# Two mixture-of-experts stages and what stands between them: order of scores, routing, biases and projections

## The chip, the cores and the metric

The kernel runs on one core of a Trainium2 chip: TensorE (PE, with its weight loads PEld), VectorE (DVE), ScalarE (ACT), GpSimd (POOL), and SyncE (SP), which issues most transfers. The metric is the device time of one execution in microseconds. The kernel before has a median of 1687.51 us over three runs (1680.59 to 1689.58).

## The reference, cut to what matters

Eight layers run one after the other on 2048 tokens of 128 features in float32, each on the output of the one before: a state-space block, 32 experts, causal attention, eight experts, windowed attention, a linear layer with ternary weights, a test-time-training block, seven experts with a shared one. Ahead of each layer the rows are normalised. The parts the change touches:

```
# eight experts, capacity 160, one expert a token
probs = softmax(x @ router_w + router_b); e = argmax(probs)
tokens of e that fit:  relu(x @ w1[e] + b1[e]) @ w2[e] + b2[e]
left-over tokens:      relu(x @ ow1 + ob1) @ ow2 + ob2
# ternary layer
y = x @ sign_with_threshold(weight).T * alpha + bias
# test-time training (Ttt): queries, keys, values by one projection,
# two gradient steps on a small gated network, then the queries through it
# seven experts, the two best of each token, plus a shared expert
w, idx = top_k(softmax(x @ router_w), 2), made to sum to 1
y = sum_k w_k * (silu(x @ w_gate[idx_k]) * (x @ w_up[idx_k])) @ w_down[idx_k]
    + (silu(x @ sw_gate) * (x @ sw_up)) @ sw_down
```

## The kernel before, in words

Every stage is a class with one method for each engine (pe, dve, act, pool, sp). The engines run their own lists of instructions in the order written out by hand and meet on semaphores. Waits.wait_ge puts a wait in an engine's list; mark and own are the waits of DVE and POOL on their own earlier results. The 2048 tokens are 16 tiles of 128 rows, handled as four chunks of four tiles. At each stage's start ChunkNorm (line 349) takes roots on ACT, a reciprocal and three tiles a chunk on DVE (line 369) and the fourth tile on POOL; ChunkFeatures (line 401) transposes a chunk on PE (line 418) into one of two PSUM banks and ACT copies it (line 428), so that tokens lie along the free axis. A float32 matmul shows as two instructions on PE.

**Eight experts (Moe8).** PE transposes all four chunks, waits for the ends of the stage before and makes the 16 score matmuls into bank 2 (line 2562). DVE adds the router bias, takes the largest score and subtracts it (2590 to 2595), ACT takes Exp (2681), DVE sums, divides, finds the largest of each tile (max, 2604) and its index (max_index, 2607). Dispatch (line 1032) marks the chosen expert, PE counts with a triangular matrix (1051, 1052), DVE makes row numbers, and POOL scatters 16 tiles with indirect DMAs (1116) into HBM. Beside that PE runs the dense layer of the left-over tokens over all rows: hidden (2570) and output (2521), c = 0 to 3, DVE and ACT evicting. DVE adds the output to X, first a sum into tmp (2619), then one update for each tile (2624), and signals ox. Only at ox = 4 does PE turn the scattered rows (rows_pe, 2530) for the first expert; hidden_pe (2540), the ReLUs (DVE 2655, ACT 2696) and out_pe (2552) follow for eight experts, the results go back by indirect DMA.

**Ternary.** PE puts the bias into each of four banks with a matmul of one row (bias_pe, 2757), transposes chunks and adds the product of each chunk (2765). DVE adds to X and takes statistics for the next norm, chunk by chunk.

**Ttt.** PE transposes chunks 0 and 1, then makes the projections of tiles 0 to 3, transposes chunk 2, projects tiles 6 and 7, transposes chunk 3, and so on (line 3060). DVE adds the key bias (3170), ACT copies values (3352), queries (3355) and squares (3347); ACT's copy of the transposed keys of chunk 0 is line 3438, and the first gradient step begins with a Sigmoid (3365).

**Seven experts (Moe7).** The tokens of each expert are laid out in blocks of 256 rows, NB = 22 of them ("e"), and the shared expert has eight blocks ("s") over all tokens. The order of blocks is:

```
self.blocks = [("s", s) for s in range(F)] + [("e", j) for j in range(NB)] + [("s", s) for s in range(F, 8)]
```

with F = FRONT = 6, so two shared blocks stand behind the experts. The list of PE: four chunks of transposes, 16 score matmuls into bank 7 (3691), the up-projections of a block in two groups of eight instructions (3662), the down product of the block before (3674), and after the third group the two counting matmuls (3681, 3682). DVE: choose_dve (3720 to 3733) with max and max_index for each tile, place_dve (3743 to 3781) with weigh_dve inside, then the products silu(gate) * up (mul_dve, 3808) and additions to X (home_dve, 3817). For the first two blocks (EARLY = 2) ACT copies the up half out of PSUM (3873) and POOL multiplies (3919) in DVE's place, while DVE routes. POOL then issues 32 scatters (3931), SP loads the rows of a block (3606), PE turns them (3633). At the end the experts' results lie in HBM, SP reads them back in four parts (3610), DVE adds them (3826, 3828) and SP writes the output (3613).

## Time and profile before

| | |
|---|---|
| median of three runs | 1687.51 us (1680.59 to 1689.58) |
| profiled execution | 1679.48 us, its span 1677.4 us |
| TensorE granted clock, mean | 0.886 |
| busy: PE, DVE, ACT, POOL | 1264.7, 982.8, 669.4, 659.1 us |
| chain that ended last | PE 51%, DVE 13%, POOL 12%, issue 10%, DMA 6%, ACT 5%, SP's queue 3% |

Times in the rows below are counted from the span's start. Durations come from the one profiled execution. Its 2.1 us outside the span are start and end of the program. The clock column has 1.00 for 2.4 GHz and 0.50 for 1.2 GHz. "idle 2.05 <-DVE" in brackets means that the engine stood idle for so long before the instruction and that DVE ended it.

### The profile page before, as it was taken

Reading aid. Unit: us, or ns where it says so; the run is one execution under the profiler, and the core shown is the slowest. Engines: PE = TensorE matmul, PEld = TensorE weight load, DVE = VectorE, ACT = ScalarE, POOL = GpSimd, SP = SyncE. Lnnn points to the kernel's source line nnn. Section 1 sums busy time; section 2 is a strip of 40 time slices with the busy share of each in tenths; the row PEclk is TensorE's granted clock in tenths of the full one; section 3 lists DMA queues with packets and bytes.
Section 4 is the critical chain, followed back from the end, with each engine's and each line's share of the span. In section 5 each row is a group of like instructions: output and inputs, shape, how many; then the busy total and the mean of one; then the engine's idle time right before and its main releaser. Section 6 shows DMA issues by size and latency. Waiting matters only on the chain.

```text
span 1677.4 us, 23947 instructions
## 1 busy us (share of the span) xinstructions
PE 1264.7 (75%) x8790; PEld 761.1 (45%) x8790; DVE 982.8 (59%) x1746; ACT 669.4 (40%) x1253; POOL 659.1 (39%) x647
## 2 busy tenths in 40 slices
PE   5467677531684668788778489979988998994997
PEld 2123332320453224434357234445555556683997
DVE  7899899860111988878453554366545554551333
ACT  3754233120353347767722335643323323231432
POOL 1288878377576430000034200025512440054443
PEclk9679899756897769989979699989999999996999
DMA  6257568011332422211001322150000000001112
GB/s 221 104 178 265 209 232 276 18 50 51 88 94 83 163 95 68 64 47 29 9 27 30 123 92 61 38 217 4 1 0 1 0 1 1 1 25 46 48 39 92
DMA packets 75445, 133.80 MB, mean 80 GB/s; under 512 B 12723, under 2 KB 39670, under 8 KB 74688
## 3 DMA queue, kind: packets, MB, share of 16 engines
q1 hardware_dynamic: 66400, 115.97, 20.9%
q0 software_dynamic: 8064, 13.87, 2.5%
q10 hardware_dynamic: 864, 2.43, 0.4%
q8 instruction: 70, 1.15, 0.3%
q14 instruction: 47, 0.39, 0.1%
HBM read 96.22 MB, written 38.38 MB: 80 GB/s over the span
## 4 chain that ended last, share of the span: by engine, by line
PE 51%; DVE 13%; POOL 12%; issue 10%; DMA 6%; ACT 5%; SPq 3%; POOLq 0%; DVEq 0%; ACTq 0%
PE ps L3662 6%; PE ps L1752 5%; POOL sb_arena L1018 5%; POOL xe L1116 3%; PE ps L3674 3%; PE ps L2119 2%; PE ps L644 2%; DVE sb_arena L1818 2%; ACT sb_arena L2066 2%; PE ps L2102 2%; PE ps L2973 2%; PE ps L2970 2%; PE ps L2962 1%; PE ps L2964 1%; DMA sb_arena<-xe 1%
## 5 line engine op out<-in xcount | busy, mean ns | idle before, releaser
L1818 DVE TENSOR_REDUCE sb_arena<-ps 128x2 f32<-128x1024 f32 (+2 forms) x192 | 211.1, 1130 | 60.7 <-PE ps L2347 34.2
L2066 ACT ACTIVATE sb_arena<-ps 128x512 f32<-128x512 f32 (+1 forms) x320 | 160.3, 554 | 58.6 <-PE ps L2119 54.9
L644 PE MATMUL ps<-sb_arena,sb_const 128*128 128x512 f32 x256 | 136.2, 677 | 27.9 <-DVE sb_arena L837 27.9
L831 DVE TENSOR_TENSOR_SCAN sb_arena<-ps,sb_arena 128x1024 f32<-128x1024 f32 x64 | 144.9, 2279 | 4.9 <-ACT ps L926 3.9
L1850 POOL CAST sb_arena<-sb_arena 128x8 bf16<-128x8 f32 (+2 forms) x32 | 6.5, 204 | 293.1 <-DVE sb_arena L1818 149.9
L1752 PE MATMUL ps<-sb_arena 128*32 128x256 f32 (+3 forms) x1856 | 117.6, 361 | 0.4 <-ACT sb_arena L2300 0.2
L3808 DVE TENSOR_TENSOR sb_arena<-sb_arena,ps 128x512 f32<-128x512 f32 x56 | 38.4, 687 | 111.8 <-PE ps L3662 111.8
L1116 POOL DMA_INDIRECT xe<-sb_arena x80 | 79.9, 999 | 51.0 <-issue 30.5
L644 PEld LDWEIGHTS ps<-sb_arena,sb_const 128*128 128x128 f32 x256 | 56.1, 221 | 93.5 <-issue 53.5
L1018 POOL TENSOR_TENSOR sb_arena<-sb_Wreg,sb_arena 128x1024 f32<-128x1024 f32 x32 | 79.0, 2490 | 40.3 <-DMA sb_arena<-bcrows 32.1
L3514 POOL TENSOR_TENSOR sb_arena<-sb_arena 128x512 f32<-128x512 f32 x32 | 40.7, 1270 | 137.2 <-DVE sb_arena L3192 137.2
L1478 POOL DMA_INDIRECT y<-sb_arena x80 | 77.7, 972 | 37.5 <-ACT sb_arena L1432 20.1
L3662 PE MATMUL ps<-sb_arena 128*128 128x256 f32 x352 | 85.2, 385 | 0.5 <-ACT sb_arena L3855 0.5
L2119 PE MATMUL ps<-sb_arena 51*128 51x256 bf16 (+2 forms) x768 | 61.7, 253 | 28.2 <-ACT sb_arena L2066 27.8
L1018 POOL TENSOR_TENSOR sb_arena<-sb_arena 128x1024 f32<-128x1024 f32 x32 | 74.6, 2355 | 19.5 <-DMA sb_arena<-bcrows 14.8
L2102 PE MATMUL ps<-sb_arena 55*128 55x128 bf16 (+4 forms) x576 | 63.6, 298 | 18.5 <-DVE sb_arena L1818 11.9
L2300 ACT ACTIVATE sb_arena<-ps 128x768 f32<-128x768 f32 x64 | 50.3, 786 | 62.7 <-PE ps L2369 62.7
L617 PE MATMUL ps<-sb_arena,sb_constb 96*128 96x512 bf16 x96 | 31.0, 406 | 57.1 <-DVE sb_arena L837 50.4
L3940 POOL DMA_INDIRECT y<-sb_arena x44 | 43.0, 976 | 76.5 <-ACT sb_arena L3863 69.8
L3662 PEld LDWEIGHTS ps<-sb_arena 128*128 128x128 f32 x352 | 64.6, 193 | 8.5 <-ACT sb_arena L3855 0.9
L926 ACT ACTIVATE ps<-sb_arena 128x1024 f32<-128x1024 f32 x32 | 35.8, 1118 | 77.2 <-DVE sb_arena L831 77.1
L837 DVE TENSOR_TENSOR sb_arena<-sb_arena,ps 128x1024 f32<-128x1024 f32 x48 | 58.6, 1221 | 12.2 <-PE ps L617 6.1
(479 smaller groups left out, 2856.0 us busy)
## 6 DMA issues: line engine op xcount, KB each, us to landing
sb_arena<-bcrows SPq DMA_DIRECT2D x80, 512.0 KB, 6.4
xe<-sb_one SPq DMA_DIRECT2D x31, 260.0 KB, 8.9
sb_Wreg<-e0w SPq DMA_DIRECT2D x24, 256.0 KB, 7.2
sb_arena<-xe SPq DMA_DIRECT2D x16, 325.0 KB, 3.1
y<-sb_zero SPq DMA_DIRECT2D x20, 256.0 KB, 6.7
sb_arena<-y SPq DMA_DIRECT2D x4, 1024.0 KB, 9.1
sb_Wreg<-e1w SPq DMA_DIRECT2D x16, 256.0 KB, 2.7
sb_Wreg<-e3gu SPq DMA_DIRECT2D x1, 4096.0 KB, 12.5
```

The source lines that it names most:

```text
L644: t = e.matmul(k.b(self.Y + c), k.c("ident"), self.hc[i % 4][:, c * 512:(c + 1) * 512], start=False, stop=n == 15)
L831: e.tensor_tensor_scan(self.hh[i % 3], k.pair(2 * (i % 2)).rearrange("p c t -> p (c t)"), self.dB[i % 3], 0.0, MUL, ADD).then_inc(S.scan.s ...
L837: e.tensor_tensor(self.two(self.hc[i % 4]), self.two(self.hh[i % 3]), k.pair(self.C), MUL).then_inc(S.hcv.sem, 1)
L1018: e.tensor_tensor(self.dB[i % 3], self.du[b][:, eb, :], self.Bs[i % 4], MUL).then_inc(S.dB.sem, 1)
L1116: e.indirect_dma_start(buf, bass.IndirectOffsetOnAxis(self.iw[:, c:c + 1], 0), xn[q][:, i, :], None, bounds_check=rows - 1, oob_is_err=Fal ...
L1478: e.indirect_dma_start(self.y, bass.IndirectOffsetOnAxis(at, 0), self.ob[u % 3][:, c, :], None, bounds_check=8191, oob_is_err=False).then_ ...
L1752: t = e.matmul(k.b(self.sum_bank(qc))[32 * j:32 * j + 32, o:o + wd], self.vaug[:, b * 8 + kt, 4 * hg + j, :], self.PT[x][:, j, a - q0:a - ...
L1818: e.tensor_reduce(dst, src, AX.X, MAX).then_inc(S.mxr.sem, 1)
L2066: e.activation(self.PT[s % 4][:, 2 * h:2 * h + 2, 0:n], bank[:, :, 0:n], ACT.Exp, scale=self.scale).then_inc(S.ex.sem, 1)
L2102: t = e.matmul(view[:, p, a:z], Q[r, j % 2, tok], KK[r, j % 2, k0 + a:k0 + z], start=True, stop=True, skip_group_check=True)
L2119: t = e.matmul(banks[h][:, j, a:z], KK[r, j, kt * 128:(kt + 1) * 128], Q[r, j, q0 + a:q0 + z], start=True, stop=True, skip_group_check=True)
L3662: t = e.matmul(k.b(2 * (n % 2) + which)[:, 256 * q:256 * (q + 1)], self.matrix(which, block, 2 * (n % 2) + q), src, start=True, stop=True)
```

## The change

In Moe8 the scores are made chunk by chunk between the transposes, in banks 6 and 7 (half of the tiles each), and routing runs by halves: shift of half 0, its Exp and maxima, shift of half 1, indices of half 0, maxima and indices of half 1. The scores of the second half wait for signal od of the stage before. Turning rows no longer waits for ox = 4 but for the evictions of the left-over layer; hidden_pe waits for a new signal ov, the sum into tmp. ACT takes the root of chunk 3 after the first copy of features. In Ternary the bias of bank 3 moves behind the output of chunk 2. In Ttt the projections of tiles 0 to 3 go ahead of chunk 1's transposes, and ACT's copy of the keys goes ahead of the last value copy, the last query copy behind the last root. In Moe7 scores are made by chunks, in two parts of 12 and 4 tiles, and DVE chooses in these parts; PE counts right after the scores, ACT takes the Exp ahead of its copy of the rows, EARLY with its copies and POOL products goes away, and FRONT is 7.

```diff
@@ -2514,7 +2514,7 @@
         w.wait_ge(S.oha, 2 * c + 2)
-        w.wait_ge(S.ox, c - 1)
+        w.wait_ge(S.ov, c - 1)
         for j in range(4):
@@ -2524,7 +2524,8 @@
         w.wait_ge(S.rows, 16)
-        w.wait_ge(S.ox, 4)
+        w.wait_ge(S.ohv, 8)
+        w.wait_ge(S.oha, 8)
         w.wait_ge(S.xT, ex - 1)
@@ -2533,6 +2534,7 @@
         w.wait_ge(S.xT, ex + 1)
+        w.wait_ge(S.ov, 4)
         for g in range(2):
@@ -2552,15 +2554,30 @@
+    def scores(self, h):
+
+        return self.k.b(6 + h)[:, 0:8 * self.E]
+
+    def scores_pe(self, e, w, c):
+        k, E = self.k, self.E
+        self.f.wait(w, c)
+        for j in range(4):
+            i, o = 4 * c + j, (4 * (c % 2) + j) * E
+            t = e.matmul(self.scores(c // 2)[:, o:o + E], self.xnT[:, i * 128:(i + 1) * 128], k.s("rw1"), start=True, stop=True)
+        return t
+
     def pe(self, e, w):
         k, S, E = self.k, self.S, self.E
-        self.f.pe(e, w, self.ln.wait_rows)
+        self.f.chunk_pe(e, w, self.ln.wait_rows, 0)
+        self.scores_pe(e, w, 0)
+        self.f.chunk_pe(e, w, self.ln.wait_rows, 1)
+        self.f.chunk_pe(e, w, self.ln.wait_rows, 2)
+        self.scores_pe(e, w, 1).then_inc(S.lg.sem, 1)
+        self.f.chunk_pe(e, w, self.ln.wait_rows, 3)
         w.all(self.before.ends)
-        lg = k.b(2)[:, 0:NT * E]
-        for i in range(NT):
-            self.f.wait(w, i // 4)
-            t = e.matmul(lg[:, i * E:(i + 1) * E], self.xnT[:, i * 128:(i + 1) * 128], k.s("rw1"), start=True, stop=True)
-        t.then_inc(S.lg.sem, 1)
+        w.wait_ge(self.before.S.od, 16)
+        self.scores_pe(e, w, 2)
+        self.scores_pe(e, w, 3).then_inc(S.lg.sem, 1)
         self.disp.pe(e, w)
@@ -2582,29 +2599,50 @@
+    def half(self, h):
+
+        tiles = slice(8 * h, 8 * h + 8)
+        return tiles, self.p.rearrange("p (i e) -> p i e", e=self.E)[:, tiles], lambda v: v[:, tiles].unsqueeze(2).to_broadcast([128, 8, self.E])
+
+    def shift_dve(self, e, w, h):
+        S, E = self.S, self.E
+        tiles, p3, bc = self.half(h)
+        w.wait_ge(S.lg, h + 1)
+        w.mark(e.tensor_tensor(p3, self.scores(h).rearrange("p (i e) -> p i e", e=E),
+                               self.k.s("rb1").unsqueeze(1).to_broadcast([128, 8, E]), ADD))
+        w.own()
+        w.mark(e.tensor_reduce(self.mx[:, tiles], p3, AX.X, MAX))
+        w.own()
+        e.tensor_tensor(p3, p3, bc(self.mx), SUB).then_inc(S.shift.sem, 1)
+
+    def best_dve(self, e, w, h):
+        S = self.S
+        tiles, p3, bc = self.half(h)
+        w.wait_ge(S.probs, h + 1)
+        w.mark(e.tensor_reduce(self.sm[:, tiles], p3, AX.X, ADD))
+        w.own()
+        w.mark(e.reciprocal(self.sm[:, tiles], self.sm[:, tiles]))
+        w.own()
+        w.mark(e.tensor_tensor(p3, p3, bc(self.sm), MUL))
+        w.own()
+        for i in range(8):
+            t = e.max(self.v8[:, 8 * h + i, :], p3[:, i, :])
+        w.mark(t)
+
+    def which_dve(self, e, w, h):
+        tiles, p3, bc = self.half(h)
+        w.own()
+        for i in range(8):
+            t = e.max_index(self.i8[:, 8 * h + i, :], self.v8[:, 8 * h + i, :], p3[:, i, :])
+        w.mark(t)
+
     def route_dve(self, e, w):
...
+        self.shift_dve(e, w, 0)
+        self.best_dve(e, w, 0)
+        self.shift_dve(e, w, 1)
+        self.which_dve(e, w, 0)
+        self.best_dve(e, w, 1)
+        self.which_dve(e, w, 1)
         w.own()
@@ -2616,9 +2654,9 @@
         w.own()
-        w.mark(e.tensor_tensor(self.tmp.rearrange("p (j d) -> p j d", j=4), bo.rearrange("p (j d) -> p j d", j=4),
-                               self.b2[:, 1024:1152].unsqueeze(1).to_broadcast([128, 4, 128]), ADD))
-        w.own()
+        e.tensor_tensor(self.tmp.rearrange("p (j d) -> p j d", j=4), bo.rearrange("p (j d) -> p j d", j=4),
+                        self.b2[:, 1024:1152].unsqueeze(1).to_broadcast([128, 4, 128]), ADD).then_inc(S.ov.sem, 1)
+        w.wait_ge(S.ov, c + 1)
         for j in range(4):
@@ -2674,11 +2712,16 @@
         k, S = self.k, self.S
-        self.ln.act(e, w, self.before.S.stats, (2, 3))
-        self.f.act(e, w)
+        ready = self.before.S.stats
+        self.ln.act(e, w, ready, (2,))
+        self.f.chunk_act(e, w, 0)
+        self.ln.act(e, w, ready, (3,))
+        for c in range(1, 4):
+            self.f.chunk_act(e, w, c)
         w.all(self.before.ends)
-        w.wait_ge(S.shift, 1)
-        e.activation(self.p, self.p, ACT.Exp).then_inc(S.probs.sem, 1)
+        for h in range(2):
+            w.wait_ge(S.shift, h + 1)
+            e.activation(self.p[:, 64 * h:64 * h + 64], self.p[:, 64 * h:64 * h + 64], ACT.Exp).then_inc(S.probs.sem, 1)
         for c in range(4):
@@ -2775,13 +2818,13 @@
         self.bias_pe(e, 2)
-        self.bias_pe(e, 3)
         self.f.chunk_pe(e, w, self.ln.wait_rows, 1)
...
         self.out_pe(e, w, 2)
+        self.bias_pe(e, 3)
         self.out_pe(e, w, 3)
@@ -3062,10 +3105,10 @@
         self.f.chunk_pe(e, w, self.ln.wait_rows, 0)
-        self.f.chunk_pe(e, w, self.ln.wait_rows, 1)
         w.wait_ge(S.g_w, 16)
...
         self.qkv_pe(e, w, range(0, 4))
+        self.f.chunk_pe(e, w, self.ln.wait_rows, 1)
         self.f.chunk_pe(e, w, self.ln.wait_rows, 2)
@@ -3432,11 +3475,11 @@
         self.root_act(e, w, 2)
-        self.value_act(e, w, 3)
-        self.query_act(e, 3)
         w.wait_ge(S.ktp, 1)
         e.copy(self.kT[:, 0:512], k.b(0)).then_inc(S.kT.sem, 1)
+        self.value_act(e, w, 3)
         self.root_act(e, w, 3)
+        self.query_act(e, 3)
         for step in range(2):
@@ -3548,7 +3591,9 @@
-    BLK, NB, FRONT, EARLY = 256, 22, 6, 2
+    BLK, NB, FRONT = 256, 22, 7
+
+    PARTS = [(0, 12, 4), (12, 16, 5)]
     ROWS = BLK * NB
...
@@ -3653,9 +3697,7 @@
             src = self.xT[m % 3]
-        if 2 <= n < 2 + 2 * self.EARLY:
-            w.wait_ge(S.uc, n - 1)
-        elif n >= 2:
+        if n >= 2:
             self.wait_h(w, n - 2)
@@ -3681,15 +3723,27 @@
+    def scores_pe(self, e, w, c):
+
+        k = self.k
+        self.f.wait(w, c)
+        bank = k.b(self.PARTS[c // 3][2])
+        for i in range(4 * c, 4 * c + 4):
+            t = e.matmul(bank[:, i * 8:(i + 1) * 8], self.xnT[:, i * 128:(i + 1) * 128], k.s("rw3"), start=True, stop=True)
+        return t
+
     def pe(self, e, w):
         k, S = self.k, self.S
-        self.f.pe(e, w, self.ln.wait_rows)
+        self.f.chunk_pe(e, w, self.ln.wait_rows, 0)
+        self.f.chunk_pe(e, w, self.ln.wait_rows, 1)
+        self.scores_pe(e, w, 0)
+        self.f.chunk_pe(e, w, self.ln.wait_rows, 2)
+        self.scores_pe(e, w, 1)
+        self.scores_pe(e, w, 2).then_inc(S.lg.sem, 1)
+        self.f.chunk_pe(e, w, self.ln.wait_rows, 3)
+        self.scores_pe(e, w, 3).then_inc(S.lg.sem, 1)
         w.all(self.before.ends)
-        lg = k.b(7)[:, 0:128]
-        for i in range(NT):
-            self.f.wait(w, i // 4)
-            t = e.matmul(lg[:, i * 8:(i + 1) * 8], self.xnT[:, i * 128:(i + 1) * 128], k.s("rw3"), start=True, stop=True)
-        t.then_inc(S.lg.sem, 1)
+        self.count_pe(e, w)
         w.wait_ge(k.g_w["e3"], 32)
@@ -3700,8 +3754,6 @@
                 self.turn_pe(e, w, self.blocks[v + 1][1])
-            if v == 1:
-                self.count_pe(e, w)
             self.up_pe(e, w, 2 * v + 1)
@@ -3716,18 +3768,19 @@
         v8, i8 = self.v8, self.i8
-        w.wait_ge(S.lg, 1)
...
+        for x, (a, z, bank) in enumerate(self.PARTS):
+            w.wait_ge(S.lg, x + 1)
+            w.mark(e.tensor_copy(self.p[:, 8 * a:8 * z], k.b(bank)[:, 8 * a:8 * z]))
+            w.own()
+            w.mark(e.tensor_copy(p3[:, a:z, 7], k.c("padneg").to_broadcast([128, z - a])))
+            w.own()
+            for i in range(a, z):
+                t = e.max(v8[:, i, :], p3[:, i, :])
+            w.mark(t)
+            w.own()
+            for i in range(a, z):
+                t = e.max_index(i8[:, i, :], v8[:, i, :], p3[:, i, :])
+            w.mark(t)
         w.own()
@@ -3834,12 +3887,10 @@
         last = len(self.blocks)
-        for v in range(self.EARLY):
-            self.home_dve(e, w, v)
-        for v in range(self.EARLY, last):
+        for v in range(last):
             for n in (2 * v, 2 * v + 1):
                 self.mul_dve(e, w, n)
-            if v > self.EARLY and self.blocks[v - 1][0] == "s":
+            if v and self.blocks[v - 1][0] == "s":
                 self.home_dve(e, w, v - 1)
@@ -3868,15 +3919,19 @@
         e.activation(self.sg[y], k.b(2 * y), ACT.Silu).then_inc(S.sg.sem, 1)
-        if n < 2 * self.EARLY:
-            w.wait_ge(S.mu, n + 1)
-            e.copy(self.uc[y], k.b(2 * y + 1)).then_inc(S.uc.sem, 1)
...
         k, S = self.k, self.S
-        self.ln.act(e, w, self.before.S.stats)
-        self.f.act(e, w)
+        ready = self.before.S.stats
+        self.ln.act(e, w, ready, (0, 1, 2))
+        self.f.chunk_act(e, w, 0)
+        self.f.chunk_act(e, w, 1)
+        self.ln.act(e, w, ready, (3,))
+        self.f.chunk_act(e, w, 2)
+        self.f.chunk_act(e, w, 3)
         w.all(self.before.ends)
+        w.wait_ge(S.shift, 1)
+        e.activation(self.d, self.d, ACT.Exp).then_inc(S.probs.sem, 1)
         self.ln.wait_rows(w, 3)
@@ -3885,9 +3940,6 @@
             self.silu_act(e, w, 2 * v)
-            if v == 0:
-                w.wait_ge(S.shift, 1)
-                e.activation(self.d, self.d, ACT.Exp).then_inc(S.probs.sem, 1)
             if more and v >= self.FRONT:
@@ -3911,13 +3963,6 @@
             e.tensor_copy(self.xq[q].bitcast(I32)[:, :, 128], k.c("places").rearrange("p (i q) -> p q i", q=2)[:, q]).then_inc(S.ids.sem, 1)
-        for n in range(2 * self.EARLY):
-            v, y = n // 2, n % 2
-            w.wait_ge(S.sg, n + 1)
-            w.wait_ge(S.uc, n + 1)
-            w.wait_ge(S.o, v - 2)
-            e.tensor_tensor(self.h[v % 3][:, 2 * y:2 * y + 2, :], self.sg[y].rearrange("p (q t) -> p q t", q=2),
-                            self.uc[y].rearrange("p (q t) -> p q t", q=2), MUL).then_inc(S.hp.sem, 1)
         self.ln.wait_rows(w, 3)
```

## Rows read from the trace of the kernel before

**Rows 1.** Chain that ended last, routing of the eight experts: start, length, what

```profile
846.47 6.64 PE ps L2562 x32
...
858.07 2.28 DVE sb_arena L2607 x17
```

**Rows 2.** Timeline there: start, length, engine, line, operation, [idle before <-releaser]

```profile
853.23 0.29 DVE L2590 TENSOR_TENSOR sb_arena<-ps,sb_small 128x128 f32<-128x128 f32 x1 [7.73 <-PE ps L2562]
...
854.27 1.28 ACT L2681 ACT_TABLE_LOAD   x1 [7.18 <-DVE sb_arena L2595]
855.57 0.31 ACT L2681 ACTIVATE sb_arena<-sb_arena 128x128 f32<-128x128 f32 x1
...
856.84 1.19 DVE L2604 MAX8 sb_arena<-sb_arena 128x8 f32<-128x8 f32 x16
...
892.84 1.14 DVE L2624 SCALAR_TENSOR_TENSOR sb_X<-sb_arena,sb_X 128x128 f32<-128x128 f32 x4
...
894.12 0.47 PE L2530 MATMUL ps<-sb_const,sb_arena 80*128 80x80 f32 x4 [2.05 <-DVE sb_X L2624]
...
895.69 0.67 DVE L2655 TENSOR_SCALAR sb_arena<-ps,sb_small 128x160 f32<-128x160 f32 x2 [1.71 <-PE ps L2540]
```

**Rows 3.** Windows, ternary stage: stretch, length, busy times, TensorE clock, DMA share, GB/s

```profile
1092.00:1094.00 2.00, 2.00 (x4) 0.65 (x2) 1.90 (x12) 0.36 (x2) 1.38 (x2) 0.50 0.00 0
```

**Rows 4.** Timeline of the ternary stage and the start of Ttt

```profile
1091.29 3.52 PE L2757 MATMUL ps<-sb_Wreg,sb_const 1*128 1x512 f32 x4
...
1092.35 1.01 DVE L369 TENSOR_SCALAR sb_Wreg<-sb_X,sb_ln,sb_rs 128x128 f32<-128x128 f32 x3
...
1094.75 1.11 PE L418 MATMUL ps<-sb_const,sb_Wreg 128*128 128x128 f32 x4
...
1105.65 1.10 PE L418 MATMUL ps<-sb_const,sb_arena 128*128 128x128 f32 x4 [2.07 <-DVE sb_arena L369]
...
1114.78 0.69 DVE L3170 TENSOR_TENSOR sb_arena<-ps,sb_small 128x512 f32<-128x512 f32 x1 [3.61 <-PE ps L3060]
...
1122.49 0.61 ACT L3438 COPY sb_arena<-ps 128x512 f32<-128x512 f32 x1
```

**Rows 5.** Timeline of the seven experts, up to the first rows turned

```profile
1467.22 1.35 PE L418 MATMUL ps<-sb_const,sb_arena 128*128 128x128 f32 x8 [2.12 <-DVE sb_arena L369]
...
1468.41 4.96 PE L3691 MATMUL ps<-sb_small,sb_arena 128*128 128x8 f32 x32
...
1478.22 0.42 DVE L3746 TENSOR_REDUCE sb_arena<-sb_arena 128x128 bf16<-128x256 f32 x1
...
1480.80 0.29 DVE L3749 COPY sb_arena<-ps 128x128 f32<-128x128 f32 x1 [0.94 <-PE ps L3682]
...
1481.66 3.94 POOL L3919 TENSOR_TENSOR sb_arena<-sb_arena 128x512 f32<-128x512 f32 x3 [2.35 <-ACT sb_arena L3873]
...
1481.98 1.11 DVE L3757 TENSOR_TENSOR sb_arena<-sb_arena 128x128 f32<-128x128 f32 x1
...
1488.26 1.11 POOL L3931 DMA_INDIRECT xe<-sb_arena  x1 [2.66 <-DVE sb_arena L3774]
...
1533.22 0.66 PE L3633 MATMUL ps<-sb_const,sb_arena 128*128 128x128 f32 x2 [25.54 <-DMA sb_arena<-xe]
...
1534.35 3.78 PE L3662 MATMUL ps<-sb_arena 128*128 128x256 f32 x8 [0.46 <-ACT sb_arena L3855]
```

**Rows 6.** Chain that ended last, the two blocks behind the experts

```profile
1658.46 6.91 PE ps L3662 x32
1665.37 3.58 PE ps L3674 x32
```

**Rows 7.** Timeline of the end

```profile
1664.60 2.01 SPq L3610 DMA_DIRECT2D sb_arena<-y  x4
...
1669.32 0.68 DVE L3826 TENSOR_TENSOR sb_X<-sb_X,sb_arena 128x512 f32<-128x512 f32 x1
```

**Rows 8.** Source line 3610, the four reads of expert rows at the end

```profile
DMA to landing us min/median/max: 3.9/5.4/6.8
```

More of the change, by code:

```diff
@@ L2470, in __init__ @@
         self.S = S = k.signals(
-            g_w=16, stats=4, ids=1, **chunk_signals(), **dispatch_signals(), lg=1, shift=1, probs=1,
-            scat=256, oh=16, ohv=8, oha=8, od=4, ox=4, rows=16, tr=8, xT=8, mg=16, hv=16, ha=16, o=8, oa=8, row0=64, row1=64, row2=64, row3=64, back0=16, back1=16, back2=16, back3=16)
+            g_w=16, stats=4, ids=1, **chunk_signals(), **dispatch_signals(), lg=2, shift=2, probs=2,
+            scat=256, oh=16, ohv=8, oha=8, od=4, ov=4, ox=4, rows=16, tr=8, xT=8, mg=16, hv=16, ha=16, o=8, oa=8, row0=64, row1=64, row2=64, row3=64, back0=16, back1=16, back2=16, back3=16)
         self.put = [S.row0, S.row1, S.row2, S.row3]
@@ L2602, in route_dve @@
         w.own()
-        for i in range(NT):
-            w.mark(e.max(self.v8[:, i, :], p3[:, i, :]))
-        w.own()
-        for i in range(NT):
-            w.mark(e.max_index(self.i8[:, i, :], self.v8[:, i, :], p3[:, i, :]))
+        for i in range(8):
[3 more added lines that the diff above has]
+        tiles, p3, bc = self.half(h)
+        w.own()
+        for i in range(8):
+            t = e.max_index(self.i8[:, 8 * h + i, :], self.v8[:, 8 * h + i, :], p3[:, i, :])
+        w.mark(t)
+    def route_dve(self, e, w):
+        self.shift_dve(e, w, 0)
[4 more added lines that the diff above has]
+        self.which_dve(e, w, 1)
         w.own()
@@ L3562, in __init__ @@
         self.S = S = k.signals(
-            **chunk_signals(), lg=1, shift=1, probs=1, chosen=1, cnt=1, eid=1, iw=1, gu=NB, dn=NB, ids=2, wts=2, xq=1, scat=512,
-            **{f"load{i}": 16 * ((NB + 5 - i) // 6) for i in range(6)}, tr=NB, xT=NB, mg=60, mu=60, sg=60, uc=2 * self.EARLY, hp=2 * self.EARLY, h=60 - 2 * self.EARLY, o=30, oa=2 * NB, ox=8,
+            **chunk_signals(), lg=2, shift=1, probs=1, chosen=1, cnt=1, eid=1, iw=1, gu=NB, dn=NB, ids=2, wts=2, xq=1, scat=512,
+            **{f"load{i}": 16 * ((NB + 5 - i) // 6) for i in range(6)}, tr=NB, xT=NB, mg=60, mu=60, sg=60, h=60, o=30, oa=2 * NB, ox=8,
             **{f"row{i}": 32 * ((NB + 3 - i) // 4) for i in range(4)}, **{f"back{c}": 16 for c in range(4)}, fin=4, out=64)
@@ L3586, in __init__ @@
         self.xT = [A.take(256) for _ in range(3)]
-        self.sg, self.uc = [A.take(512) for _ in range(2)], [A.take(512) for _ in range(2)]
+        self.sg = [A.take(512) for _ in range(2)]
         self.h = [B.take(1024).rearrange("p (b t) -> p b t", b=4) for _ in range(3)]
@@ L3615, in wait_h @@
     def wait_h(self, w, n):
-        early = 2 * self.EARLY
-        w.wait_ge(*((self.S.hp, n + 1) if n < early else (self.S.h, n + 1 - early)))
+        w.wait_ge(self.S.h, n + 1)
     def wait_out(self, w, v):
@@ L3718, in choose_dve @@
         v8, i8 = self.v8, self.i8
-        w.wait_ge(S.lg, 1)
-        w.mark(e.tensor_copy(self.p, k.b(7)[:, 0:128]))
-        w.own()
-        w.mark(e.tensor_copy(p3[:, :, 7], k.c("padneg").to_broadcast([128, NT])))
-        w.own()
-        for i in range(NT):
-            t = e.max(v8[:, i, :], p3[:, i, :])
-        w.mark(t)
-        w.own()
-        for i in range(NT):
-            t = e.max_index(i8[:, i, :], v8[:, i, :], p3[:, i, :])
-        w.mark(t)
+        for x, (a, z, bank) in enumerate(self.PARTS):
[11 more added lines that the diff above has]
+            w.mark(t)
         w.own()
```

11 lines of the change are left out of this document (removed).

## The prediction

> **What bounds the kernel now.** I read the chain that ended last, stage by stage, then the timeline where the diff touches it, then the end. One core runs the stages in a row and the chain hardly leaves them, so what counts is how much earlier each touched stretch hands on. In the stage of eight experts PE makes 32 passes of scores (two for each of 16 matmuls) after all transposes, 6.64 us, and DVE then routes until 860.35 [rows 1] with PE idle. The stage of seven experts has the same pattern: 4.96 us of scores, DVE's routing, the first of 32 scatters on POOL at 1488.26, and PE, out of work, waits 25.54 us for the rows that it turns at 1533.22 [rows 5]. The path there is scores, routing, POOL, DMA, not PE. At the end two blocks of the shared expert run on PE while the rows are read back [rows 6, 7].
>
> **Eight experts, scores and routing.** A pass took 6.64 / 32 = 0.21 us [rows 1]. Eight passes now fall into PE's wait for chunk 1's rows, eight more go between the transposes of chunks 2 and 3, where some 0.6 us of waiting was; the last score is ready 1.66 + 0.6 = 2.2 us sooner, near 850.9, the first half's near 846.9. DVE starts there: three operations of at most 0.29 us [rows 2], 0.8. The Exp waits for ACT's last copy of features, which moves to about 848.1 (846.9 with 0.6 each for chunk 3's transposes and the copy), and for its table, 1.28 [rows 2]; it ends at 849.65. From then DVE works without a wait: sum, reciprocal, product and eight maxima 1.35 (16 maxima took 1.19 [rows 2]), the second half's shift 0.8, eight indices 1.15 (half of 2.28 [rows 1]), the second half's product and maxima 1.35, its indices 1.15. That is 5.8 us, to 855.5, where it was 860.35. Eight more small instructions are in it. Bounds: 2.2 (halving pays nothing beyond the earlier scores) and 5.5 (half the width, less time). I take **4.7**. The 16 scatters and the left-over tokens' layer start earlier by the same. The new wait of the scores for signal od costs nothing: those copies are over before the last transposes.
>
> **Rows turned early.** PE stood 2.05 us between the last left-over product and the transposes, for DVE's sum and its four updates of X; the first hidden matmul came 0.7 later [rows 2]. Now PE turns at 892.1, and only the hidden layer waits for the sum, which ended at 892.8: 2.0 us earlier. But the updates (1.14 us from 892.84) stand ahead of DVE's first ReLU, which moves from 895.69 to 894.0 only [rows 2]. I take **1.7**, bounds 0 and 2.0.
>
> **Ternary stage.** Biases 2 and 3, four passes, took 3.52 us ahead of chunk 1's transposes at 1094.75 [rows 4]; its rows were ready at 1093.4 (DVE's three, 1.01 us from 1092.35 [rows 4]). With bias 2 alone (half, 1.76) PE turns then. Bias 3 moves behind output 2, where DVE's additions and statistics are the bound. PE ran at half its clock here [rows 3], so chunk 1's output may come 0.2 late. I take **1.2**, bounds 0.5 and 1.4.
>
> **Ttt stage.** The first eight passes of the projections stood behind chunk 1's transposes at 1105.65, before which PE was idle for 2.07, and need only chunk 0 [rows 4]. Its transposes ended at 1105.65 - 2.07 = 1103.6; with ACT's copy of 0.6 the passes start at 1104.2, 1.4 before chunk 1. Its transposes come later than now, but chunk 2's (the next wait for DVE) do not, and the keys of chunk 1 follow from 1114.78 [rows 4] on the same path. Bounds 0.5 and 2.5. The copy of kT (0.61 us [rows 4]) goes ahead and the query copy last; PE and the sigmoid's table now wait for that one. It costs 0.2, at most 0.6, at best nothing. Net **1.2**.
>
> **Seven experts, up to the scatters.** Before chunks 2 and 3 PE stood idle for 2.12 us; the scores ended at 1473.37, a pass costing 0.155 [rows 5]. Eight passes (1.2 us) go into that hole and chunk 2's transposes start 0.8 earlier, since ACT no longer has the last root ahead of chunk 0's copy: last score near 1471.4, first 24 passes near 1469.2. DVE takes 12 tiles first: copies 0.45, maxima 0.9, indices 1.7 (by the 1.19 and 2.28 for 16 [rows 1, 2]), to 1472.4, then four tiles with their copies in 1.5, to 1473.9 instead of 1477.5. So the reduce at 1478.22 [rows 5] moves by 3.6, its result from 1478.64 to 1475.05. DVE went on only at 1480.80 [rows 5], since the counting matmuls stood behind three groups of up-projections. Now PE counts at once, and what comes last is the Exp: shift 1474.25, table 1.28, Exp and three weight operations 0.9, so 1476.5: **4.3** gained. Behind it an addition of 128 elements took 1.11 us [rows 5] where such an operation takes 0.29 [rows 2], and two more like it (1.13, 1.25) ended with POOL's products, three in 3.94 us [rows 5]. The change takes these products off POOL: 3.49 - 0.87 = **2.6**, bounds 0 and 2.8. The first scatter moves 6.9 us, to 1481.4, and all up to 1533.22 with it, to 1526.3.
>
> Cover for the seven front blocks: DVE starts their products behind its routing, so PE pauses after two groups until 1481.8. A block is (6.91 + 3.58) / 2 = 5.24 us [rows 6]; six and a last product end near 1515, 11 us before the rows land.
>
> **The end.** One block less behind the experts takes 5.24 us off PE, but the rows' reads were issued at 1664.60 [rows 7] and landed 3.9 to 6.8 us later [rows 8]: the first at 1668.5, and the first addition ran at 1669.32 [rows 7]. The reads become the bound. I take **0.4**, bounds 0 and 0.8.
>
> **Where the skill speaks against it.** The activation began 0.02 us after its table load of 1.28 [rows 2]. The Trainium skill, "ScalarE: Activation LUTs", What ACT_TABLE_LOAD costs, puts a switch of tables at about 2.66 us with a drain. By that both Exps, which would end DVE's last wait, came 1.4 later and the sum would be 13.3 instead of 16.1; the row decides.
>
> **Sum.** 4.7 + 1.7 + 1.2 + 1.2 + 6.9 + 0.4 = 16.1 us, against the profiled execution's 1679.48: 1663.4. The runs shown have the median 1687.51 and lie from 1680.59 to 1689.58, so the profiled one is as fast as the fastest. From the median the sum gives 1671.4, from the middle of all four executions (1684.0) 1667.9; I forecast 1670. About 0.5% (8.4 us) is what a measurement here can tell from no change.
>
> **Rivals.**
> - The last block pays in full (5.2 instead of 0.4): 1665. For it: PE was the chain to 1668.95. Against: the landing at 1668.5. Chance 0.07.
> - A faster clock: PE, busier ahead of each routing, is not cut to half (the rows at 1534.35 took 3.78 for eight passes, 1.73 at full clock [rows 5, 6]). Three such stretches of 4 to 5 us give 2 each: 1664. Against: PE still idles 6 us and more in each. 0.10.
> - Half gains: the split pays only the 2.2, and POOL's products were not what stretched DVE: 16.1 - 2.5 - 2.6 = 11, so 1676. For it, the halves' handovers between ACT and DVE. 0.14.
> - The change does not do what it says: DVE gets the first scores only when ACT and PE are nearly through, another wait (copy of the rows for POOL, now behind the Exp) holds the scatters. 5 to 8 us left: 1681. The copy starts at 1475.8, 4 us ahead of its need. 0.07.
> - Slower: the front blocks become the bound. They must end by 1526.3, which a mean of over 6.7 us a block breaks. At half clock a block takes 11 us (3.78 for eight passes [rows 5], the down product doubled): 7 x 5.8 us more, less the 11 spare, puts 30 us on the forecast: 1700. Against: before, the same blocks ran on at 5.24 after pauses of 1 us. The Trainium skill, "TensorE: Matmul & The Clock Gate", A second HAM failure mode: psum-queue depth-cycling, has the clock swing when PE idles briefly between groups; by that rule this case is the outcome. 0.03.
>
> My forecast keeps 0.59. Faster by over 0.5%: 0.59 + 0.07 + 0.10 + 0.14 less some spread of the runs, 0.88; same 0.09; slower 0.03. The range 1657 to 1682 reaches from the faster rivals on a fast run to half gains on a slow one.
>
> **What would show it.** After: DVE's first routing operation of the eight experts starts before the scores end, and DVE has no wait over 1 us after the Exp; first rows turned right behind the last left-over product; three short additions of 0.29 instead of 1.1; first scatter about 7 us earlier within its stage; PE's idle time ahead of the rows near 11 instead of 25.5; additions at the end waiting for the DMA. Wrong would be: PE at work on shared blocks when the rows land, or a scatter that waits for ACT.

## The result, and the profile after

The changed kernel took 1658.22 us, median of four runs (1655.43 to 1661.09), against 1684.05 for the kernel before (four runs): ratio 0.9856, 95% interval 0.9828 to 0.9885. The forecast was 1670 with a range of 1657 to 1682. The gain is 24 to 26 us where the steps sum to 16. The profiled execution took 1655.43, its span 1653.6 (before: 1679.48 and 1677.4), mean clock 0.892 instead of 0.886.

To find where it came from, the same instruction is looked up in both traces at each stage's seam, and the starts subtracted. What changes from one seam to the next is that stretch's part. In the table "third" is a later trace of the same changed kernel (after_third, below); both stand against the one trace of before.

| stretch | forecast | first trace | third |
|---|---|---|---|
| start to causal attention (code unchanged) | 0 | +0.8 | +3.2 |
| causal attention (unchanged) | 0 | -6.7 | +1.0 |
| eight experts, scores and routing | -4.7 | -4.4 | -4.3 |
| its rows turned | -1.7 | -1.9 | -2.0 |
| window attention (unchanged) | 0 | -2.8 | +1.6 |
| ternary | -1.2 | -0.9 | -0.8 |
| start of Ttt | -1.2 | -0.8 | -1.5 |
| seven experts up to the first scatter | -6.9 | -6.7 | -7.7 |
| end | -0.4 | -1.0 | -1.0 |
| sum of the changed parts | -16.1 | -15.7 | -17.3 |

Small rests between the stretches (up to 0.6) are left out. So the parts came close to the forecast, except the end. The rest of the first trace's 23.9 us, some 8, lies in stages that the change does not touch.

The timeline of the changed kernel in the eight experts, where before all scores stood behind all transposes [rows 1, 2]; columns are start, duration, engine and line, operation, and in brackets the idle time before it with its releaser:

```profile
839.52 1.71 PE L2566 MATMUL ps<-sb_small,sb_arena 128*128 128x8 f32 x8
841.37 0.22 DVE L2611 TENSOR_TENSOR sb_arena<-ps,sb_small 128x64 f32<-128x64 f32 x1 [1.74 <-PE ps L2566]
841.97 3.42 PE L2566 MATMUL ps<-sb_small,sb_arena 128*128 128x8 f32 x16
842.22 0.59 ACT L428 COPY sb_arena<-ps 128x512 f32<-128x512 f32 x1 [1.87 <-PE ps L418]
842.82 1.28 ACT L2724 ACT_TABLE_LOAD   x1
844.11 0.26 ACT L2724 ACTIVATE sb_arena<-sb_arena 128x64 f32<-128x64 f32 x1
844.40 0.22 DVE L2622 TENSOR_REDUCE sb_arena<-sb_arena 128x8 f32<-128x64 f32 x1 [2.30 <-ACT sb_arena L2724]
...
881.94 0.50 PE L2531 MATMUL ps<-sb_const,sb_arena 80*128 80x80 f32 x4 [1.22 <-DMA sb_arena<-xe]
```

DVE starts before the second half's scores are made, waits once, for the table and the Exp, and works without a wait from 844.40 on. The last line is the first turning of rows: what ended PE's wait there is now the load of the rows, no longer DVE's updates of X [rows 2].

The seven experts, which answers to [rows 5]:

```profile
1450.13 2.51 PE L3732 MATMUL ps<-sb_small,sb_arena 128*128 128x8 f32 x16
1452.74 0.26 DVE L3773 COPY sb_arena<-ps 128x96 f32<-128x96 f32 x1 [1.56 <-PE ps L3732]
1458.37 0.42 DVE L3799 TENSOR_REDUCE sb_arena<-sb_arena 128x128 bf16<-128x256 f32 x1
1458.93 0.26 PE L3723 MATMUL ps<-sb_arena,sb_constb 128*128 128x128 bf16 x1 [2.80 <-DVE sb_arena L3799]
1459.59 0.17 DVE L3841 TENSOR_SCALAR sb_arena<-sb_arena 128x16 f32<-128x16 f32 x1 [0.80 <-ACT sb_arena L3934]
1461.36 0.28 DVE L3810 TENSOR_TENSOR sb_arena<-sb_arena 128x128 f32<-128x128 f32 x1
1464.89 1.10 POOL L3976 DMA_INDIRECT xe<-sb_arena  x1 [13.49 <-DVE sb_arena L3827]
1510.15 0.66 PE L3677 MATMUL ps<-sb_const,sb_arena 128*128 128x128 f32 x2 [13.08 <-DMA sb_arena<-xe]
```

PE now makes the scores of 12 of the 16 tiles ahead of the last chunk's transposes (the first line is the second and third chunk's), DVE's wait for the Exp is 0.80, the addition that took 1.11 us takes 0.28, the counts no longer stand behind up-projections, and PE waits 13.08 us for the rows instead of 25.54. Seven blocks fit ahead of them.

The end, answering to [rows 7]: the reads are issued at 1641.03, and DVE waits for them with no work left on PE. SPq is SP's queue.

```profile
1639.95 2.02 PE L3716 MATMUL ps<-sb_Wreg,sb_arena 128*128 128x128 f32 x16 [0.90 <-DVE sb_arena L3861]
1641.03 2.01 SPq L3655 DMA_DIRECT2D sb_arena<-y  x4
1644.94 0.69 DVE L3879 TENSOR_TENSOR sb_X<-sb_X,sb_arena 128x512 f32<-128x512 f32 x1 [2.51 <-DMA sb_arena<-y]
```

The causal attention, in four stretches. First the kernel before, then the changed one (stretch, its length, then busy time and instructions of PE, PEld, DVE, ACT and POOL, granted clock, DMA share, GB/s):

```profile
592.00:620.00 28.00, 19.41 (x170) 7.50 (x169) 23.54 (x27) 10.08 (x19) 8.00 (x14) 0.50 0.38 125
700.00:727.00 27.00, 22.61 (x263) 10.55 (x254) 18.81 (x30) 15.55 (x32) 1.62 (x8) 0.75 0.12 37
```

```profile
592.00:620.00 28.00, 18.07 (x181) 7.17 (x182) 24.98 (x29) 11.33 (x22) 9.10 (x14) 0.59 0.38 129
700.00:727.00 27.00, 21.12 (x305) 11.31 (x309) 22.34 (x34) 18.74 (x38) 1.62 (x8) 1.00 0.18 56
```

In the same 27 us PE got through 305 instructions instead of 263: before, it had been cut to 1.2 GHz for part of the stretch, after, it ran at 2.4 GHz throughout. This gave 4.5 us, and the earlier return to 2.4 GHz near 615 gave 2.2: the starts of PE's matmuls shift at these two places and at no other in the stage. The code there is the same, so the question for the runs was whether this belongs to the program.

### The profile page after: what moved, and what is told of

It reads as the page before. It is cut to its first block, busy times and chain, and to the rows that moved or that the text cites. A ratio compares the mean times of both kernels' runs of the same rounds, so it can differ in the third digit from the quotient of the medians.

```text
span 1653.6 us, 23951 instructions
## 1 busy us (share of the span) xinstructions
PE 1258.6 (76%) x8790; PEld 759.5 (46%) x8790; DVE 987.0 (60%) x1758; ACT 666.1 (40%) x1249; POOL 651.7 (39%) x643
## 4 chain that ended last, share of the span: by engine, by line
PE 49%; DVE 14%; POOL 12%; issue 11%; DMA 6%; ACT 5%; SPq 3%; POOLq 0%; DVEq 0%; ACTq 0%
PE ps L1752 5%; PE ps L3704 5%; POOL xe L1116 4%; POOL sb_arena L1018 3%; PE ps L644 3%; DVE sb_arena L1818 3%; PE ps L3716 2%; PE ps L2119 2%; ACT sb_arena L2066 2%; DVE sb_arena L831 2%; PE ps L2102 2%; DMA sb_arena<-xe 2%; PE ps L3016 2%; PE ps L3013 2%; PE ps L3005 1%
## 5 line engine op out<-in xcount | busy, mean ns | idle before, releaser
L1752 PE MATMUL ps<-sb_arena 128*32 128x256 f32 (+3 forms) x1856 | 113.0, 350 | 0.4 <-ACT sb_arena L2300 0.2
```

What stands on the lines that cost most here:

```text
L1752: t = e.matmul(k.b(self.sum_bank(qc))[32 * j:32 * j + 32, o:o + wd], self.vaug[:, b * 8 + kt, 4 * hg + j, :], self.PT[x][:, j, a - q0:a - ...
```

## The experiments

Theories: **P**, the change speeds the untouched stages; **U**, they swing from execution to execution. There are twelve runs, in three groups of four; each group had one chip for all its kernels, named B, C and D below. A stands for the result and the first two traces, whose chip is not on record.

**Chip B: both kernels again.** before_again and after_again have no edit.

> The kernel before, unchanged, for a second trace. In the first two traces the causal attention, whose code the change does not touch, took 7.1 us less after the change (its clock fell for some 15 us near 712 before, and did not after) and the window attention 2.8 us less. Theory U (these stages swing from run to run, and the parts that were changed give only 15 to 16 us): this trace shows a causal attention that differs from the first one's 224.8 us (608.5 to 833.3) by several us. Theory P (it goes with the program): 224.8 within 1.5 us again. Ratio 1.000 within 0.3%.

> The changed kernel, for a second trace. Theory P: causal attention 218.1 us again (within 1.5), total 24 to 26 us below the kernel before. Theory U: causal attention anywhere from 218 to 225, and a total of 15 to 26 us below. The changed stretches themselves should repeat within 0.5 us each: 4.4 routing of eight experts, 1.9 rows turned, 1.7 ternary and start of Ttt, 6.7 seven experts up to the scatters, 0.9 end.

Measured: before_again 1713.62 (ratio 0.9999, interval 0.9976 to 1.0021); after_again 1704.12 against 1712.06, ratio 0.9953 (0.9923 to 0.9982). The gain fell from 24 us to 8, and both kernels are slower than on A, by 30 and by 46 us. Neither theory had this. The trace of after_again shows why, beside the scatters of the seven experts:

```profile
1507.13 0.60 ACT L3921 ACTIVATE sb_arena<-ps 128x512 f32<-128x512 f32 x1 [3.65 <-PE ps L3704]
1507.27 0.97 POOL L3976 DMA_INDIRECT xe<-sb_arena  x1 [0.30 <-issue]
1524.00 0.37 PE L3716 MATMUL ps<-sb_Wreg,sb_arena 128*128 128x128 f32 x1 [1.72 <-issue]
1526.10 0.37 PE L3716 MATMUL ps<-sb_Wreg,sb_arena 128*128 128x128 f32 x1 [1.73 <-issue]
1528.90 0.37 PE L3716 MATMUL ps<-sb_Wreg,sb_arena 128*128 128x128 f32 x1 [2.42 <-issue]
1537.32 0.42 DVE L3870 TENSOR_TENSOR sb_X<-sb_X,ps 128x256 f32<-128x256 f32 x1 [27.27 <-remote]
1539.47 1.08 ACT L3921 ACTIVATE sb_arena<-ps 128x512 f32<-128x512 f32 x2 [31.74 <-remote]
1558.65 0.38 PE L3677 MATMUL ps<-sb_const,sb_arena 128*128 128x128 f32 x2
```

PE needs 2 to 3 us for each matmul of 0.37 us, with no releaser ("issue"); DVE's addition had its input since 1505.6 and ran at 1537.32. POOL's scatters go on at their 1.28 us. This **crawl** begins 13 to 20 us behind the first scatter (1494.37) and ends within 6 us of the last. In the first trace after the change the same stretch has nothing of the kind. PE therefore had four of its seven front blocks unfinished when the rows were there, and turned them at 1558.65, 19.3 us later against the first scatter than in the trace of before. before_again pays only 2.9 us at this place, so on this chip the changed kernel loses 16.4 us to it here: its six blocks start further ahead of the scatters, so that only the last was still open when the rows came:

```profile
1548.62 3.75 PE L3662 MATMUL ps<-sb_arena,sb_Wreg 128*128 128x256 f32 x8 [7.49 <-issue]
1567.58 3.78 PE L3662 MATMUL ps<-sb_arena,sb_Wreg 128*128 128x256 f32 x8 [15.21 <-DVE sb_arena L3808]
1573.67 0.38 PE L3633 MATMUL ps<-sb_const,sb_arena 128*128 128x128 f32 x2
```

The crawl also stands beside the indirect DMAs of the 32 experts (23 us in before_again, 17 of them beside those that carry the results back) and of the eight experts (9 us), which the change hardly alters.

The causal attention took 222.9 us in before_again and 218.1 in after_again, where the first two traces have 224.8 and 218.1. The first lies 1.9 from the earlier trace, just outside the 1.5 that theory P allowed; the second fits both theories.

**Chip B: the two large parts alone.** only_moe8 is the kernel before with the new Moe8, only_moe7 with the new Moe7.

> Only the part in the stage of eight experts is made (scores by chunks, routing by halves, rows turned early). By the sum of parts 4.4 + 1.9 = 6.3 us faster, ratio 0.9963. Theory P, if what speeds the untouched stages comes with this part: 14 to 16 us faster, ratio 0.991, with a causal attention near 218 us. Theory U: between 6 and 16, the excess being just what the causal and the window attention show against the first trace of before.

> Only the part in the stage of seven experts is made (scores by parts, count at once, Exp last, products on DVE, seven front blocks). By the sum of parts 6.7 + 0.9 = 7.6 us faster, ratio 0.9955; with the products on DVE the three short additions take 0.3 us each instead of 1.1. Theory P, if the speed of the untouched stages comes with this part: 15 to 17 us faster. Theory U: 7 to 17, the excess seen in the attentions.

Measured: only_moe8 1705.58, ratio 0.9949 (0.9915 to 0.9984), 6.5 us less by the medians and 8.7 by the ratio; only_moe7 1717.62, ratio 1.0033 (1.0006 to 1.006), 5.6 us slower. Against before_again on the same chip, the second gains 7.8 us from the stage's start to its first scatter, and then turns its rows 16.4 us later against that scatter: on this chip the change to the seven experts is a loss. The causal attention took 221.8 and 224.6 us, so neither part brings the 218 of theory P.

**Chip C: the changed kernel again, and three undone steps.**

> The changed kernel once more, as the measure for the three others of this call, and to see whether chips differ. On the chip of the second call both kernels took 1700 us and more: beside the scatters (the indirect DMAs that POOL issues) PE, DVE and ACT ran one instruction per 1 to 3 us, from 14 us behind the first scatter until the last, and the change won 8 us instead of 26. Theory C (it goes with the chip): where the kernel before takes 1680 to 1690, no such crawl is in this trace and the ratio is 0.984 to 0.987; where it takes 1710, the crawl is there and the ratio 0.994 to 0.997. Theory T (it comes and goes on any chip): the two kernels' runs of one call spread over both levels.

Measured: 1665.33 against 1687.14, ratio 0.9867 (0.9835 to 0.9898), with no crawl in the trace. Theory C fits: no run lies at the other level of its group. Each chip was used at one time only, so chip and time can't be told apart. The causal attention took 225.8 us here, one more than in the trace of before: theory P fell.

pool_back gives POOL its products back:

```
 FRONT, EARLY = 7, 2
 for n in range(2 * self.EARLY):
     w.wait_ge(S.sg, n + 1)
     w.wait_ge(S.uc, n + 1)
     e.tensor_tensor(self.h[...], self.sg[y], self.uc[y], MUL).then_inc(S.hp.sem, 1)   # on POOL
```

> The changed kernel with the products of the first two shared blocks given back to POOL (and their up-projections copied out by ACT for it). Theory S (POOL's products stretch DVE's short operations, and stand ahead of the scatters): one or more of DVE's placing operations take 1.1 us instead of 0.3, and the first scatter comes 2.6 to 4 us later than in the changed kernel; total 2.6 to 4 us slower on a chip without the crawl. Rival R (the 1.1 us had another cause, and POOL is free in time): no placing operation over 0.5 us, first scatter within 0.5 us, same total.

```profile
1473.49 0.18 DVE L3830 CAST sb_arena<-sb_arena 128x32 int32<-128x32 f32 x1
1473.64 2.60 POOL L3979 TENSOR_TENSOR sb_arena<-sb_arena 128x512 f32<-128x512 f32 x2 [11.50 <-ACT sb_arena L3929]
1473.90 0.29 DVE L3834 TENSOR_REDUCE sb_arena<-sb_arena 128x22 f32<-128x132 f32 x1
1474.23 0.81 DVE L3836 TENSOR_SCALAR sb_arena<-sb_arena 128x22 int32<-128x22 f32 x1
1478.12 1.27 POOL L3979 TENSOR_TENSOR sb_arena<-sb_arena 128x512 f32<-128x512 f32 x1 [0.46 <-ACT sb_arena L3929]
1479.55 1.10 POOL L3991 DMA_INDIRECT xe<-sb_arena  x1 [0.17 <-issue]
```

The row numbers (the CAST) are ready at 1473.67, the first scatter comes at 1479.55, behind POOL's four products: 4.9 us later than in after_third, counted from the stage's start, and more than the 2.6 to 4 expected. Median 1669.27, 3.9 more than after_third, though the two intervals overlap (0.9861 to 0.9929 against 0.9835 to 0.9898). The cost here is POOL's queue, not DVE: only one small operation was stretched (0.81 instead of 0.18), since the products came when DVE was nearly through. It ended at 1475.03, POOL's first product at 1475.00. So the stretch itself was still to be shown (products_dve).

front6 sets FRONT = 6 in the changed kernel.

> The changed kernel with six shared blocks ahead of the experts and two behind them, as before the change. Without the crawl: theory L (the last reads bound the end, PE has no say there) gives 0.4 to 0.9 us slower, since PE has 11 us to spare ahead of the first rows and so gains nothing from the missing block; the rival (the block counts in full behind the experts) gives 5.2 us slower. With the crawl a front block does not fit in ahead of the rows, so it is paid there too: then it is 4.3 to 4.8 us faster than the changed kernel by theory L, and the same by the rival.

Median 1664.86, against 1665.33: the same within the runs, so only the trace speaks here. In its trace the end comes 1.0 us later than in after_third, counted from the last turned rows; the reads were issued at 1651.23, the first addition ran at 1656.15, 4.92 later instead of 3.91. Theory L held, a little over its size: a block that costs PE 5.24 us is worth 1.0 at the end.

whole_routing keeps the early scores, but routes 16 tiles at once:

```
-        self.shift_dve(e, w, 0); self.best_dve(e, w, 0); self.shift_dve(e, w, 1) ...
+        for h in range(2):
+            w.wait_ge(S.lg, h + 1)   # add the bias, half by half
+        # then one maximum, one Exp, one sum, 16 max, 16 max_index, as before
```

> The changed kernel, but the stage of eight experts routes all 16 tiles at once, behind its last score; scores are still made by chunks and rows are still turned early. My theory (halves fill the waits for the last scores, for the table load and the Exp, and make 2.2 of the 4.4 us): the first scatter of that stage 2.0 to 2.6 us later than in the changed kernel, total 2 to 2.6 us slower. Rival (the eight extra small instructions and the handovers eat the halves' gain, the early scores did it all): within 0.7 us.

```profile
853.41 0.23 DVE L2608 TENSOR_TENSOR sb_arena<-ps,sb_small 128x64 f32<-128x64 f32 x1 [3.83 <-PE ps L2566]
854.45 1.28 ACT L2703 ACT_TABLE_LOAD   x1 [3.67 <-DVE sb_arena L2613]
856.09 0.29 DVE L2615 TENSOR_REDUCE sb_arena<-sb_arena 128x16 f32<-128x128 f32 x1 [1.74 <-ACT sb_arena L2703]
```

Routing ended 2.5 us later than in after_third, counted from the stage's start; median 1668.98, 3.6 more, again with overlapping intervals (0.9853 to 0.9919 against 0.9835 to 0.9898). DVE's 3.83 us for the last score and 1.74 for the table are what the halves fill. The early scores alone keep 1.8 of the 4.3.

**Chip D: the stretch, the rows, the parts again.** This chip has the crawl too.

> The kernel before, with the products of the first two shared blocks on DVE instead of POOL (no copies by ACT for them); the counting matmuls stand one group of up-projections earlier, since that group now waits for DVE. Theory S (POOL's products stretched three of DVE's placing operations from 0.3 to 1.1 and 1.25 us): all placing operations at 0.2 to 0.45 us, 2.6 us saved, and up to 1.0 more because DVE gets the counts earlier: first scatter 2.6 to 3.6 us earlier within the stage, total faster by the same. Rival R (something else stretched them, such as ACT's or PE's traffic): the three operations still take over 1 us each, and the first scatter moves by 1.0 at most.

```
-            if v == 1:
-                self.count_pe(e, w)          # behind the third group
+        mul_dve for v = 0, 1 too; no uc, no hp; count_pe ahead of the third group
```

```profile
1505.38 0.42 DVE L3748 TENSOR_TENSOR_SCAN sb_arena<-sb_const,sb_arena 128x128 f32<-128x128 f32 x1
1506.24 0.28 DVE L3754 TENSOR_TENSOR sb_arena<-sb_arena 128x128 f32<-128x128 f32 x1
1506.55 0.17 DVE L3756 TENSOR_TENSOR_SCAN sb_arena<-sb_const,sb_arena 128x8 f32<-128x8 f32 x1
1506.96 0.29 DVE L3760 SCALAR_TENSOR_TENSOR sb_arena<-sb_arena 128x128 f32<-128x128 f32 x1
```

The three operations fell from 1.11, 1.13 and 1.25 us to 0.28, 0.17 and 0.29, and the first scatter came 2.8 us earlier within the stage than in only_moe8_2, which has the old stage on the same chip, and as much earlier against the counts: theory S held, and the earlier counts gave nothing. Yet the kernel is 0.3% slower than before (1716.4, ratio 1.003, 1.0003 to 1.0057): its front blocks start later by their products, meet the crawl sooner, and the rows are turned 58.4 us behind the first scatter, where only_moe8_2 takes 46.8.

rows_wait undoes the early turning:

```
-        w.wait_ge(S.ohv, 8)
-        w.wait_ge(S.oha, 8)
+        w.wait_ge(S.ox, 4)
```

> The changed kernel, with the turning of the rows in the stage of eight experts waiting for the sum of the left-over tokens again. My step: the first rows turned 1.7 to 2.0 us later, total 1.7 slower. Rival (the rows' load, which landed 5.1 us after its issue and ended the wait in the changed kernel's chain, is now what PE waits for): the rows turned less than 0.7 us later, total the same.

```profile
923.53 1.14 DVE L2661 SCALAR_TENSOR_TENSOR sb_X<-sb_arena,sb_X 128x128 f32<-128x128 f32 x4
924.82 0.47 PE L2530 MATMUL ps<-sb_const,sb_arena 80*128 80x80 f32 x4 [2.05 <-DVE sb_X L2661]
```

PE is idle for 2.05 us again, where only_moe8_2 on the same chip turns its rows at 915.56 with no wait behind the left-over layer. The step is worth 2.0 to 2.2: from the last left-over product's start to the first turned rows it is 9.36 us here and 7.14 in only_moe8_2. From the stage's first scatter the distance is 4.2 us longer (38.0 and 33.9); the other 2 us lie in the crawl ahead of that product, where traces of one kernel part differ by as much. The rival has a share: on chip A the load ended 1.22 us of waiting, on chip C 0.21, on D none, so it caps the step where the left-over layer is early. Ratio 0.9985 (0.9959 to 1.0011); the changed kernel itself was not timed on this chip, so this median has nothing to stand against.

> Only the part of the eight experts, again, on the chip of this call. Where the chip shows no crawl beside the scatters: 4.4 + 1.9 = 6.3 us faster by the sum of parts, ratio 0.9963. If the changed kernel's 22 to 26 us on such chips hold more than its parts (about 16), one of the two partial kernels must win clearly more than its own parts: over 9 us here.

> Only the part of the seven experts, again, on the chip of this call. Without the crawl: 6.7 to 7.7 up to the scatters and 0.9 to 1.2 at the end, 8 us faster, ratio 0.9953; on the chip with the crawl it was 0.33% slower, since its front blocks had not run ahead of the rows. A chip without the crawl on which this kernel is not faster would refute that reading. Over 11 us faster: the untouched stages gain with this part.

Measured: 1703.23, ratio 0.996 (0.9932 to 0.9987), and 1717.08, ratio 1.0041 (1.0014 to 1.0068): as on chip B. The causal attention took 224.7 us in the first and 218.1 in the second, on one chip, with the same code. On chip B the two ratios and the 2 us of ternary and Ttt add up to 5 us where the whole change gave 8, which the intervals of 3 to 6 us each allow. No partial kernel was timed on a chip without the crawl, so that their gains there add up is read from traces, not timed.

**Theories P and U.** Over all fourteen traces the causal attention lies between 218.1 and 225.8 us, though all fourteen kernels are the same up to its end; on chip D alone it has 218.1 and 225.8. The changed kernel itself has 218.1, 218.1 and 225.8; the kernels with the old eight experts have 224.8, 222.9, 224.6, 220.6 and 218.1. It goes with neither program nor chip: U holds for the traces. What stays open is a part of the medians. On chips A and C they differ by 25.8 and 21.8 us, and the changed parts explain 16 to 17; the one trace of before there is its fastest execution. Its others fall into two clusters, 1679.9 to 1681.1 and 1687.1 to 1690.2, and the cause of the 7 us between them is not known. On chip C their mean clock is 0.877 to 0.881, that of the changed kernel 0.884 to 0.887, and that of the one trace of before 0.886. The clock may be part of it, but it does not separate the two clusters, and no slower execution of before was traced there.

## Why the prediction was right, and where it was not

- **Scores and routing of the eight experts**, 4.7: 4.4 and 4.3. The split of the sum held too: halves 2.5 by whole_routing, scores 1.8 where I had 2.2. DVE got the Exp 0.6 later than worked out: ACT's last copy of features (842.22 to 842.81), which the table load waits for as I had said, came that much later. The load took 1.28 us again and the Exp began 0.01 behind it, so the 2.8 us by which the sum would have been 13.3 were not paid.
- **Rows early**, 1.7: 1.9 to 2.2. I had taken off 0.3 for the updates of X; they fit beside the hidden layer.
- **Ternary and Ttt**, 1.2 and 1.2: 0.8 to 0.9, and 0.8 to 1.5. Not tried alone.
- **Seven experts**, 6.9: 6.7 and 7.7, of which products_dve gives 2.8 to the stretch (2.6 forecast; I had put 0.29 for the scan of 8 columns too, which takes 0.17). The Trainium skill, "SBUF — State Buffer", SBUF: two separate sides, says that VectorE and GpSimd share a pair of ports as an exclusive lock, taken by a VectorE operation with two inputs in SBUF or in a two-port mode. The trace agrees: the three stretched operations have two such inputs and end 0.15, 0.04 and 0.15 us behind a product of POOL, while a reduction with one took 0.22 us at 1481.84, in the middle of POOL's product. Two inputs are not needed: the operation stretched in pool_back, a TENSOR_SCALAR, has one. No run shows in which mode it ran. The price that I had missed is the other one: in pool_back the products held the scatters for 4.9 us.
- **The end**, 0.4: 1.0, and 1.0 by front6. The reads bound it, as said, but before the change the first addition came 4.72 us behind their issue [rows 7], and now 3.91. This is the one term that was less than half of what it measured.
- **The total** came out 12 us below 1670. The sum's steps are not to blame for it: the parts hold, and in the profiled execution the rest is the swing of untouched stages. For the median that is not shown. I had put nothing for such a swing beyond the spread of the runs, so that 1658 still lies in a range that ends at 1657 is partly luck. The rival of a faster clock gave nearly this time (1664), but by another mechanism: it placed the gain in the touched stretches, and 7 of the 8 us lie in an attention ahead of all of them. In the touched stretches the clock still fell: to 1.2 GHz for 17 us in the routing of the eight experts. The sum of the half-gains rival is 1675, not 1676.
- **The rival that I gave 0.03** is what happens on chips B and D. I had written that the front blocks must end before the rows land and that PE then has 11 us to spare. In the first trace they ended 13.1 us ahead, at 2.4 GHz from 1465 to 1502. I named half the clock as what could break it. It was broken by the crawl: four blocks were unfinished, and the rows were turned 19.3 us late. On chip B the change is worth 0.5% instead of 1.4%, and its part in the seven experts is a loss of 0.33 and 0.41% on B and D. The forecast held because the chip of the result has no crawl; nothing in the profile of before shows a crawl, but the 11 us were one cover for one assumption and deserved more than 0.03.

## What to carry to other kernels

Work placed in the shadow of a long DMA phase is only free while the engines run at speed there; leave slack by the slowest chip, and place the order so that what the phase's end waits for is done first. Small operations on DVE that work from SBUF to SBUF do not belong on a critical path beside POOL's products (0.17 us became 1.13), and a product on POOL delays every DMA that POOL must issue behind it: count its queue. When a median moves more than the parts do, subtract the traces at every seam before explaining it, and take a second trace on another chip.

## What the runs showed of the hardware that was not expected

- **The crawl.** In two of the four places (B and D) PE, DVE and ACT slow to one instruction per 1 to 3 us beside a row of indirect DMAs issued by POOL, in every kernel, the old one too, and in all three expert stages: 23, 9 and 3 us in before_again. On A and C it is absent from all six traces. The runs of before say the same: 1679 to 1690 on A and C, 1702 to 1723 on B and D, with nothing between. The scatters themselves are not slower: from the first to the last of the seven experts' 32 it is 39.7 us in after_again and 40.5 in the first trace after. The Trainium skill, "Runtime: NRT & Kernel Launch", Instruction fetch mechanics, says that each engine fetches its code in blocks by a DMA queue of its own, mostly hidden. The trace does not settle whether that is starved here: two small instruction transfers lie in 1505 to 1510 of after_again, 12 and 15 us behind the first scatter, where the crawl begins, and none in the 30 us of the crawl itself. But the first trace after has the same two, 11 and 15 us behind its first scatter, and no crawl. In the eight experts PE's first gap of over 0.9 us comes 17.0 to 17.1 us behind the first scatter in all eight traces of B and D, and no instruction transfer begins in the 9 us before it. So the start of the crawl goes with the scatters. Its cause was not tried. Every timed run here comes with its span and clock, so it was recorded as well, and no run shows these kernels without a recording.
- **The clock's dip** in the causal attention comes and goes between executions of one program and is worth 4.5 us in one place: the 27 us around 712 had 0.75 in the trace of before, 0.79 in after_third and 1.00 in the first trace after.
